# Query rows split into two 16-bit halves and turned by DMA instead of on TensorE, in an attention and feed-forward kernel

## The chip, the cores and the metric

The kernel runs on one core of one Trainium2 chip. The metric is the device time of one execution in microseconds (us), the median of several runs. The engines are TensorE (PE, with its weight loads listed as PEld), VectorE (DVE), ScalarE (ACT), GpSimd (POOL) and SyncE (SP), which only issues transfers here.

## The reference, cut to what matters

```python
# 4 batches of 256 rows, D = 256; context: 4 batches of 1601 rows
q = (xn @ wq).reshape(B, L, 16, 128)        # xn: layer norm of x
k, v = xn @ wk, xn @ wv                     # 4 key/value heads of 128
q, k, k_ctx = rms_norm(q), rms_norm(k), rms_norm(ctx @ wk_ctx)
q, k = rope(q), rope(k)                     # rotary embedding, own rows alone
scores = q @ concat(k_ctx, k).T * scale + causal_mask
out = softmax(scores) @ concat(v_ctx, v) @ wo
# then x + out, a quantised feed-forward part, a second attention, a mixture of experts
```

All products are wanted at more than 16-bit accuracy, so the kernel holds each operand as the sum of a high and a low float16 part (names ending in _h and _l) and makes a product from three matmuls.

## The kernel before

**Groups and units.** The attention of the first layer is worked off in 16 groups (batch times key/value head, `NG`). A group has 8 units (`UNITS`): 4 heads times 2 tiles of 128 query rows. One unit is 128 query rows of one head against 1601 context keys and 128 or 256 own keys. In unit u of a group TensorE makes the scores of unit u + 2 (`qk`, lines 1217 to 1219 called with `qT_h`, `kT_h`) and the product with the values of unit u (`pv`, lines 1365, 1366 and 1369). In between stands the softmax: DVE takes the row maximum (`chunk_max` line 1722, `row_max` lines 1728 and 1730), ACT takes the exponential (`exp`, line 1517), ACT and POOL round it to the high half (`p_hi`, POOL's `split_last`), DVE and POOL subtract to get the low half (`p_lo`, line 1742), and SP turns both halves by DMA (`turn`, lines 1157 and 1160, target `pT_h` and `pT_l`).

**Jobs.** The operands of the next group are made between these steps. `JOBS_AT` is a list written out by hand: for each unit the jobs that run in it, in order. `("piece", p)` projects two tiles of context (or the own rows: pieces 0 and 1 are the query rows of the two tiles, 2 the own keys and values, 3 the last 65 context rows). `("kq", s)` turns normalised rows on TensorE as float32 transposes through PSUM; steps 1 to 3 are 512 context keys each, 4 the last 65, 5 the own 256 keys, 0 and 6 the query rows of tile 0 and 1 (line 1307). ACT then copies the high half from PSUM (`kq_hi_part`, line 1504) and DVE subtracts the low half (`kq_lo_part`, lines 1716 and 1718). `("out", i)` is the output projection of the group before. On PE the first job of a unit comes before the scores, the others after them; on ACT two jobs come after `p_hi` and the rest behind; on DVE the first job stands between the two halves of `p_lo`, the second after them, the rest behind.

**PSUM banks.** Jobs take three banks in turn (`XBS`), so a job waits on PE until the third job before it has been read out (`bank_user`, `wait_bank`). All engines run in program order; there is no other scheduler.

**POOL** normalises the rows and applies the rotary embedding (`POOL_AT`): the query rows of tile 0 in unit 0, those of tile 1 in units 1 and 2, own keys in unit 3, context keys behind.

**SP's queue** carries, in program order, the two turns of each unit, and between them loads for the weights of later stages (`lane_load` after unit 0, one load after unit 3, two stores of 128 KB after unit 7). The context of two of the four batches is held in SBUF; the other two wait in DRAM, and `bring_back` reloads one of them at the end of group 2 and one at the end of group 6, as two transfers of 800 KB each.

Before the groups there is a preparation phase (`PREP_JOBS`, the jobs of group 0, with rotary embedding and norms on DVE), before that the context summary of the second layer, and behind the groups a tail of about 200 us which the change does not touch.

Of the kernel before, what the change touches and what calls it, by code (L numbers as in the profile page):

```python
# [63 lines left out]
KQ_STEPS = 7  # L64
# [11 lines left out]
OUT_JOBS = [j for j in JOB_LIST if j[0] == "out"]  # L76
# [5 lines left out]
KQ_AT = {s: [j for j in PREP_JOBS if j[0] == "kq"].index(("kq", s)) for s in range(KQ_STEPS)}  # L82
# [91 lines left out]
def build(nc, x, ctxT, wq, wk, wv, wo, wk_ctx, wv_ctx, q_norm, k_norm, w_gateT, w_upT, w_downT,  # L174
# [3 lines left out]
    with ExitStack() as ctx:  # L178
# [73 lines left out]
        sq = sm("sq", [P, 2, REP, DH], BF16)  # L252
# [3 lines left out]

        kT_h = sm("kT_h", [P, 2, KEY_COLS], F16)
# [113 lines left out]
        ot_tr, ot_hi, ot_lo, oj_mm, x1_done = (sem(n) for n in ("ot_tr", "ot_hi", "ot_lo", "oj_mm", "x1_done"))  # L371
        dve_step, act_step = sem("dve_step"), sem("act_step")
# [98 lines left out]

        def squares_at(p):

            return sum(piece_slots(k) for k in range(p))
# [14 lines left out]
        def kq_view(s, kT, qT, par, bank):  # L489

            if s in (0, 6):
                lt = s // 6
                return qT[:, par, lt * REP:(lt + 1) * REP, :].rearrange("p h n -> p (h n)"), PS[:, bank, :], False
# [8 lines left out]

        def prep_bank(n):
            return PREP_BANKS[n % len(PREP_BANKS)]

        def job_bank(job):
            return XBS[JOB_LIST.index(job) % len(XBS)]
# [12 lines left out]

        def bank_user(job, g):

            kind, i = job
            if kind == "mean":
                return (("kq", 3), NG - 1) if i == 0 else (("mean", 0), g)
            at = JOB_LIST.index(job) - len(XBS)
            while g >= 0:
                if at < 0:
                    at, g = at + len(JOB_LIST), g - 1
                elif runs(JOB_LIST[at], g):  # L530
                    return JOB_LIST[at], target(JOB_LIST[at], g)
                else:
                    at -= len(XBS)
            return None
# [53 lines left out]
        def run_job(g, job, kinds):  # L588

            kind, i = job  # L590
            if kind == "mean":
                kinds[kind](i)
            elif kind == "out":
                kinds[kind](i, target(job, g), job_bank(job))
            else:
                to = target(job, g)
                kinds[kind](i, to, to % 2, job_bank(job))
# [530 lines left out]
        def _(sp):  # L1128
# [32 lines left out]

            def group(g, last=False):
                for u in range(UNITS):
                    turn(g, u)
                    if u == 0 and 0 < g < NG - 1:
                        lane_load(g)
                    if u == LANE_AT + 1 and g < NG - 1:
                        sp.wait_ge(lane_sum, g + 1)
                        sp.dma_start(piece_f.rearrange("p (c n) -> p c n", c=kept_sources[g].shape[1]), kept_sources[g])\
                          .then_inc(pw_in, 16)  # L1170
                    if u == UNITS - 1 and g < NG - 1:
                        sp.wait_ge(pw_lo, g + 1)
                        for k, t in enumerate((piece_h, piece_l)):
                            sp.dma_start(kept_w[k, :, g * KEPT:(g + 1) * KEPT], t).then_inc(pw_kept, 16)
# [14 lines left out]
            def bring_back(slot, groups_done):  # L1189

                sp.wait_ge(pc_mm, NP * groups_done)
                for k, t in enumerate((ctx_h, ctx_l)):
                    sp.dma_start(t[:, slot, :, :].rearrange("p c n -> p (c n)"), kept[slot, k, :, :])\
                      .then_inc(ctx_moved, 16)

            lane_load(0)
            for g in range(NG):
# [13 lines left out]
        def _(pe):  # L1211
# [61 lines left out]
            def piece(p, g, par, bank=XB):  # L1273

                b, kv = g // KVH, g % KVH
                kind = PIECES[p]
                if p == KV_PIECES[0]:
                    pe.wait_ge(ctx_moved, 64 + 64 * (g // (2 * KVH)))
                if kind in ("q0", "q1"):
                    lt = int(kind[1])  # L1280
                    jobs = [(PS[:, bank, :], xT_h, xT_l, (b * L + lt * P), P, wsf_h, wsf_l, 0, 512)]
                elif kind == "self":
                    jobs = [(PS[:, bank, lt * 256:lt * 256 + 256], xT_h, xT_l, (b * L + lt * P), P, wsf_h, wsf_l, 512, 256)
                            for lt in range(LT)]
                elif kind == "rem":
                    jobs = [(PS[0:CREM, bank, 0:256], None, None, (CT - 1) * P, CREM, wc_h, wc_l, 0, 256)]
                else:
                    jobs = [(PS[:, bank, j * 256:j * 256 + 256], None, None, (2 * kind[1] + j) * P, P, wc_h, wc_l, 0, 256)
                            for j in range(2)]
                for o, ah, al, col, n, bh, bl, w0, wn in jobs:  # L1290
                    for c in range(DC):
                        if ah is None:
                            lhs = (ctx_h[:, ds(b % SLOTS, 1), c, col:col + n].rearrange("p a n -> p (a n)"),
                                   ctx_l[:, ds(b % SLOTS, 1), c, col:col + n].rearrange("p a n -> p (a n)"))
                        else:
                            lhs = (ah[:, c, ds(col, n)], al[:, c, ds(col, n)])
                        last = three(o, lhs, (bh[:, c, kv, w0:w0 + wn], bl[:, c, kv, w0:w0 + wn]),
                                     c == 0, c == DC - 1)
                last.then_inc(pc_mm, 1)

            def transpose_kq(s, g, par, bank=XB):

                if s in (0, 6):
                    lt = s // 6
# [33 lines left out]
            def qk(g, u, c, par):  # L1338
# [43 lines left out]
            kinds = {"out": out_proj, "piece": piece, "kq": transpose_kq, "mean": mean}  # L1382
            turn, rotate, turn_first, tail = tail_pe(pe, three)

            def group(g, par, first, last):
                for u in range(UNITS):
# [19 lines left out]
                    if last and u == UNITS - 1:  # L1406
# [4 lines left out]
                        out_proj(0, NG - 1, job_bank(("out", 0)))  # L1411
# [8 lines left out]
            for n, (kind, i) in enumerate(PREP_JOBS):  # L1420
                if n == 2:
                    pe.wait_ge(l1_R, B)
                if n >= len(PREP_BANKS):
                    wait_bank(pe, PREP_JOBS[n - len(PREP_BANKS)], 0)
                to = 1 if n == len(PREP_JOBS) - 1 else 0
                kinds[kind](i, to, to, prep_bank(n))
# [9 lines left out]
            for i, before in ((1, (("out", 3), NG - 2)), (2, (("out", 0), NG - 1)), (3, (("out", 1), NG - 1))):  # L1436
                wait_bank(pe, *before)
                out_proj(i, NG - 1, job_bank(("out", i)))
# [4 lines left out]
        def _(act):  # L1443
# [39 lines left out]
            def piece_out(p, g, par, bank=XB):  # L1483
# [5 lines left out]
                wait(act, pc_copy, pieces_done(p, g) - 2)  # L1489
                act.wait_ge(pc_mm, pieces_done(p, g))  # L1490
                rows, w = (CREM if kind == "rem" else P), (DH if q else 2 * DH)
                for j in range(piece_slots(p)):
                    act.activation(sq[0:rows, p % 2, j, :], PS[0:rows, bank, j * w:j * w + DH], ACT.Square,  # L1493
# [45 lines left out]
            kinds = {"out": out_hi_part, "piece": piece_out, "kq": kq_hi_part,  # L1539
# [11 lines left out]
            def group(g, par, first, last):  # L1551

                for u in range(UNITS):
# [16 lines left out]
                    else:  # L1570
# [3 lines left out]
                        out_hi_part(0, NG - 1, job_bank(("out", 0)))  # L1574
# [18 lines left out]
            out_hi_part(1, NG - 1, job_bank(("out", 1)))  # L1593
# [4 lines left out]
        def _(dve):  # L1598
# [111 lines left out]

            def kq_lo_part(s, g, par, bank=XB):
# [80 lines left out]
            kinds = {"out": out_lo_part, "piece": piece_lo, "kq": kq_lo_part,  # L1792
# [14 lines left out]
            def group(g, par, first, last):  # L1807
                for u in range(UNITS):
# [18 lines left out]
                    if last and u == UNITS - 1:  # L1827
                        lo_part(0, 0, 0)
                        lo_part(0, 0, 1)
                        out_lo_part(0, NG - 1, job_bank(("out", 0)))  # L1830
# [50 lines left out]
            for i in range(1, 2 * LT):  # L1881
                out_lo_part(i, NG - 1, job_bank(("out", i)))
# [192 lines left out]
```

## Time and profile before

| | |
|---|---|
| median of 3 runs | 1298.2 us (1294.91 to 1299.37) |
| the profiled execution | 1299.34 us, its span 1297.5 us |
| PE busy | 1193.7 us, 92% of the span |
| PE weight loads busy | 893.8 us, 69% |
| DVE busy | 1015.4 us, 78% |
| ACT busy | 832.3 us, 64% |
| POOL busy | 790.8 us, 61% |
| mean granted TensorE clock | 0.976 |
| hardware DMA queue | 56.5% of the 16 engines |
| chain that ended last | PE 69%, DVE 16%, DMA 5% |

The profile is one execution taken by the hardware profiler. Matmuls are pipelined: a matmul's recorded duration is longer than the distance to the next one, so costs on PE are read from the distances between starts. The idle time in brackets at the end of a timeline line is the engine's idle time before that instruction, with what released it.

### The profile page before, as it was taken

To read this page: it belongs to the slowest core of one execution; us is meant where nothing else is said; L and a number is where in the kernel's file an instruction comes from. 1 tells how busy PE (TensorE), PEld (TensorE's weight loads), DVE (VectorE), ACT (ScalarE), POOL (GpSimd) and SP (SyncE) were. 2 spreads that over 40 slices of the span, in tenths; PEclk is the share of its full clock that TensorE was granted. 3 is DMA by queue.
4 is the path that set the end of the run, shared out by engine and by line. 5 is a ranking of instruction groups with operands and counts; after the bars stand their busy time and mean duration, and the time that the engine had idled before them with its cause. 6 is when DMAs were issued, how large, how long until landed. Compare 5 with 4: busy or idle time off the path is not lost.

```text
span 1297.5 us, 30487 instructions
## 1 busy us (share of the span) xinstructions
PE 1193.7 (92%) x11547; PEld 893.8 (69%) x11547; DVE 1015.4 (78%) x1979; ACT 832.3 (64%) x1917; POOL 790.8 (61%) x1010
## 2 busy tenths in 40 slices
PE   4998699999999999999999999999999976777898
PEld 2544477877787777778777777777777765455557
DVE  6876768888688888788888878888888887776673
ACT  4755567776677676767677677777777644446431
POOL 2765386867668585857668595857768533761000
PEclk9998999999999999999999999999999998789999
DMA  8620067576867687695767677676778898000000
GB/s 286 201 82 15 18 137 163 129 159 134 187 135 154 143 148 149 128 209 130 159 132 152 145 148 147 133 160 139 151 145 153 161 193 222 1 1 1 1 1 33
DMA packets 507298, 164.94 MB, mean 127 GB/s; under 512 B 485488, under 2 KB 500352, under 8 KB 506896
## 3 DMA queue, kind: packets, MB, share of 16 engines
q1 hardware_dynamic: 506128, 159.57, 56.5%
q0 software_dynamic: 1024, 3.42, 1.0%
q8 instruction: 92, 1.51, 0.5%
q14 instruction: 54, 0.44, 0.1%
HBM read 33.05 MB, written 8.26 MB: 32 GB/s over the span
## 4 chain that ended last, share of the span: by engine, by line
PE 69%; DVE 16%; DMA 5%; POOL 3%; ACT 3%; issue 3%; SPq 2%; POOLq 0%; DVEq 0%; ACTq 0%
PE PS L1217 14%; PE PS L1219 13%; PE PS L1218 13%; PE PS L1369 7%; PE PS L1365 7%; PE PS L1366 7%; DVE mx L1722 5%; DVE pl L1742 3%; DMA pT_l<-pl 2%; DMA pT_h<-ph 2%; PE PS L1318 1%; PE PS L706 1%; PE PS L684 1%; DMA sin<-in_c_sin 1%; DVE f_s L1653 1%
## 5 line engine op out<-in xcount | busy, mean ns | idle before, releaser
L1722 DVE TENSOR_REDUCE mx<-PS 128x1 f32<-128x512 f32 (+2 forms) x512 | 296.5, 622 | 123.8 <-PE PS L1219 122.6
L1365 PE MATMUL PS<-v_h,pT_h 128*128 128x129 f16 (+1 forms) x1856 | 225.8, 222 | 9.9 <-DMA pT_h<-ph 9.9
L1959 POOL CAST ph<-pr_end 128x705 f16<-128x705 f32 (+1 forms) x128 | 109.9, 858 | 200.4 <-ACT pr_end L1517 200.4
L1366 PE MATMUL PS<-v_l,pT_h 128*128 128x128 f16 (+1 forms) x1856 | 225.8, 221 | 0.0
L1365 PEld LDWEIGHTS PS<-v_h,pT_h 128*128 128x128 f16 (+1 forms) x1856 | 182.7, 98 | 14.0 <-DMA pT_h<-ph 11.3
L1217 PE MATMUL PS<-kT_h,qT_h 128*128 128x512 f16 (+2 forms) x512 | 181.9, 355 | 7.6 <-ACT pr L1517 7.6
L1517 ACT ACTIVATE pr<-PS,nb 128x1024 f32<-128x1024 f32 x128 | 144.0, 1125 | 68.9 <-DVE nb L1730 68.9
L1366 PEld LDWEIGHTS PS<-v_l,pT_h 128*128 128x128 f16 (+1 forms) x1856 | 183.0, 99 | 2.4
L1218 PE MATMUL PS<-kT_l,qT_h 128*128 128x512 f16 (+2 forms) x512 | 181.0, 354 | 0.0
L1219 PE MATMUL PS<-kT_h,qT_l 128*128 128x512 f16 (+2 forms) x512 | 180.8, 353 | 0.0
L1742 DVE TENSOR_TENSOR pl<-pr,ph 128x1024 f16<-128x1024 f32 x128 | 169.3, 1322 | 0.0
L1493 ACT ACTIVATE sq<-PS 128x128 bf16<-128x128 f32 (+1 forms) x368 | 98.9, 283 | 81.3 <-PE PS L1219 81.0
L1369 PE MATMUL PS<-v_h,pT_l 128*128 128x129 f16 (+1 forms) x1856 | 131.6, 222 | 6.7 <-DMA pT_l<-pl 6.6
L1444 ACT ACTIVATE ph<-pr 128x1024 f16<-128x1024 f32 x128 | 135.5, 1059 | 0.0
L1369 PEld LDWEIGHTS PS<-v_h,pT_l 128*128 128x128 f16 (+1 forms) x1856 | 114.5, 98 | 8.6 <-DMA pT_l<-pl 8.4
L1517 ACT ACTIVATE pr_end<-PS,nb 128x705 f32<-128x705 f32 (+1 forms) x128 | 117.4, 917 | 3.6 <-DVE pl L1742 3.6
L1217 PE MATMUL PS<-wc_h,ctx_h 128*128 128x256 f16 (+1 forms) x416 | 113.4, 273 | 3.8 <-DVE v_l L1708 3.4
L1219 PE MATMUL PS<-wc_h,ctx_l 128*128 128x256 f16 (+1 forms) x416 | 113.3, 272 | 0.0
L1218 PE MATMUL PS<-wc_l,ctx_h 128*128 128x256 f16 (+1 forms) x416 | 113.3, 272 | 0.0
L1742 DVE TENSOR_TENSOR pl<-pr_end,ph 128x512 f16<-128x512 f32 x128 | 107.9, 843 | 0.3 <-issue 0.3
L1444 ACT ACTIVATE o_s<-PS,rden 128x128 f32<-128x128 f32 x128 | 48.1, 376 | 91.5 <-DVE rden L1757 91.0
L1932 POOL TENSOR_TENSOR rs<-rs,mhalf 128x4 f32<-128x4 f32 (+2 forms) x100 | 101.7, 1016 | 7.8
(287 smaller groups left out, 2964.4 us busy)
## 6 DMA issues: line engine op xcount, KB each, us to landing
stage<-in_ctxT SPq DMA_DIRECT2D x8, 800.5 KB, 6.6
weights_kept<-relay SPq DMA_DIRECT2D x30, 128.0 KB, 2.3
relay<-in_w_lanes SPq DMA_DIRECT2D x14, 204.9 KB, 3.6
stage<-in_wq SPq DMA_DIRECT2D x4, 512.0 KB, 4.0
stage<-in_wo SPq DMA_DIRECT2D x4, 512.0 KB, 3.8
pT_h<-ph SPq DMA_TRANSPOSE x128, 3.6
pT_l<-pl SPq DMA_TRANSPOSE x128, 3.6
ctx_kept<-ctx_h SPq DMA_DIRECT2D x2, 800.5 KB, 8.1
```

What stands on the lines that cost most here:

```text
L1217: mm(o, ah, bh, start=start, stop=False)
L1218: mm(o, ah, bl, start=False, stop=False)
L1219: return mm(o, al, bh, start=False, stop=stop)
L1365: mm(PS[:, OB, 0:DH + 1], pT_h[0:rows, slot, t, :], v_h[0:rows, par, v, :], start=t == 0, stop=False)
L1366: mm(PS[:, OB, 0:DH], pT_h[0:rows, slot, t, :], v_l[0:rows, par, v, :], start=False, stop=False)
L1369: last = mm(PS[:, OB, 0:DH + 1], pT_l[0:rows, slot, t, :], v_h[0:rows, par, v, :], start=False, stop=t == len(tiles) - 1)
L1444: copy = lambda o, i, scale=1.0: act.activation(o, i, ACT.Copy, scale=scale)
L1517: act.activation(o, i, ACT.Exp, bias=nb[:, slot:slot + 1], scale=SCALE).then_inc(exp_done, 1)
L1722: dve.reduce_max(mx[:, c:c + 1], PS[:, c, 0:cols(u % LT, c)], AX_X).then_inc(mx_part, 1)
L1742: dve.tensor_tensor(pl[:, slot, at], src, ph[:, slot, at], ALU.subtract).then_inc(p_lo_made, 1)
L1932: last = pool.tensor_tensor(rs[:, 0:n], rs[:, 0:n], mhalf[:, 0:n], ALU.pow)
L1959: pool.tensor_copy(ph[:, slot, HALF:LAST + w], pr_end[:, 0:BANK + w]).then_inc(pool_hi, 1)
```

## The change

- **Query turns.** The jobs `("kq", 0)` and `("kq", 6)` are gone; in their places stand `("q", 0)` in unit 2 and `("q", 1)` in unit 4 instead of unit 3. A q job does nothing on PE. ACT copies the 128x512 float32 query rows to `qn_h` (float16), DVE subtracts to `qn_l`, and SP turns both with a DMA transpose into `qT_h` and `qT_l`, behind the turns of unit 3 and of unit 5. There is one `qn_h` and one `qn_l`: ACT waits before it overwrites them until the turns of the other tile have landed (`turned_q`). The first scores of each tile wait for `turned_q` on PE.
- **Own keys.** `("kq", 5)` moves from the end of unit 3 to the head of unit 4, and `("piece", 9)` comes behind the scores in unit 4.
- **Banks.** A group now has 19 jobs with a bank instead of 21, so the three banks rotate from group to group; each job still waits for the third before it.
- **Context reload.** `bring_back` becomes four transfers of 400 KB, one each behind units 0 to 3 of groups 3 and 7. The wait for them on PE now asks for the reload that the batch needs.
- **Squares.** The scratch tile `sq` becomes single, with a wait for the previous piece's copy (ACT's own), and a query piece waits until `qn_l` of the last use is made.

```diff
-           [("piece", 5), ("kq", 0), ("piece", 6)],
-           [("piece", 7), ("kq", 6), ("piece", 8), ("kq", 5)],
-           [("piece", 9), ("kq", 4), ("kq", 1)],
+           [("piece", 5), ("q", 0), ("piece", 6)],
+           [("piece", 7), ("piece", 8)],
+           [("kq", 5), ("piece", 9), ("kq", 4), ("q", 1), ("kq", 1)],
            [("kq", 2), ("kq", 3)],
...
+            def turn_queries(lt, g):
+                par = g % 2
+                sp.wait_ge(q_lo, g * LT + lt + 1)
+                for t, rows in ((qT_h, qn_h), (qT_l, qn_l)):
+                    sp.dma_start_transpose(t[:, par, lt * REP:(lt + 1) * REP, :], rows[:, :]).then_inc(turned_q[lt], 16)
...
                     turn(g, u)
+                    if u in (3, 5) and not last:
+                        turn_queries(u // 2 - 1, g + 1)
...
+                    if g in (KVH - 1, 2 * KVH - 1) and u < 2 * DC:
+                        bring_back(g // KVH, u)
...
+            def bring_back(slot, part):
+
+                if part == 0:
+                    sp.wait_ge(pc_mm, NP * KVH * (slot + 1))
+                t, c = (ctx_h, ctx_l)[part // DC], part % DC
+                sp.dma_start(t[:, slot, c, :], kept[slot, part // DC, :, c * SC:(c + 1) * SC]).then_inc(ctx_moved, 16)
...
-                if g in (KVH - 2, 2 * KVH - 2):
-                    bring_back(g // KVH, (g // KVH + 1) * KVH)
...
-                    pe.wait_ge(ctx_moved, 64 + 64 * (g // (2 * KVH)))
+                    pe.wait_ge(ctx_moved, 64 * max(1, g // KVH))
...
-                if s in (0, 6):
-                    lt = s // 6
-                    pe.wait_ge(rope_done, g * len(ROPES) + ROPES.index(f"q{lt}1") + 1)
-                    for j in range(REP):
-                        last = pe.transpose(PS[:, bank, j * P:(j + 1) * P], qr[:, lt * REP + j, :], ident[:, :])
-                elif s == 4:
+                if s == 4:
...
-                    pe.wait_ge(kq_lo, kq_done([[0, 1], [2], [3], [4, 5]][c], g))
-                if u == 1 and c == 0:
-                    pe.wait_ge(kq_lo, kq_done([6], g))
+                    pe.wait_ge(kq_lo, kq_done([[1], [2], [3], [4, 5]][c], g))
+                if u < LT and c == 0:
+                    pe.wait_ge(turned_q[u], 32 * (g + 1))
...
+            def q_hi_part(lt, g, par, bank=None):
+                n = g * LT + lt
+                act.wait_ge(rope_done, g * len(ROPES) + ROPES.index(f"q{lt}1") + 1)
+                wait(act, turned_q[1 - lt], 32 * ((n + 1) // 2))
+                copy(qn_h[:, :], query_rows(lt)).then_inc(q_hi, 1)
...
+            def q_lo_part(lt, g, par, bank=None):
+                dve.wait_ge(q_hi, g * LT + lt + 1)
+                dve.tensor_tensor(qn_l[:, :], query_rows(lt), qn_h[:, :], ALU.subtract).then_inc(q_lo, 1)
```

## Rows read from the trace of the kernel before

**Rows 1.** The page's part 1: busy time, share of the span, instructions, by engine.
```profile
PE 1193.7 (92%) x11547; PEld 893.8 (69%) x11547; DVE 1015.4 (78%) x1979; ACT 832.3 (64%) x1917; POOL 790.8 (61%) x1010
```

**Rows 2.** Windows: length, busy us by engine, granted clock, DMA share, GB/s.
```profile
400.00:500.00 100.00, 98.76 (x1063) 78.83 (x1061) 83.15 (x160) 73.85 (x193) 76.58 (x99) 1.00 0.71 145
...
337.00:347.00 10.00, 7.02 (x63) 5.79 (x62) 3.84 (x6) 5.46 (x19) 9.16 (x14) 0.83 0.93 200
```

**Rows 3.** PE's waits over the whole run: releaser, us in total, times, longest.
```profile
PE PS L1365 <- DMA pT_h<-ph: 9.9, 4, 4.4
...
PE PS L1314 <- DVE v_l L1708: 7.8, 15, 0.6
```

**Rows 4.** DVE's timeline (start, duration): the lane sum, once per group, unit 2.
```profile
297.90 1.27 DVE L1747 TENSOR_REDUCE relay<-relay 48x1 f32<-48x1094 f32 x1
...
360.40 1.27 DVE L1747 TENSOR_REDUCE relay<-relay 48x1 f32<-48x1094 f32 x1
...
476.20 1.27 DVE L1747 TENSOR_REDUCE relay<-relay 48x1 f32<-48x1094 f32 x1
...
534.06 1.27 DVE L1747 TENSOR_REDUCE relay<-relay 48x1 f32<-48x1094 f32 x1
...
593.84 1.27 DVE L1747 TENSOR_REDUCE relay<-relay 48x1 f32<-48x1094 f32 x1
```

**Rows 5.** PE's timeline, unit 2 of group 6: query transposes and the next job.
```profile
529.88 0.61 PE L1307 MATMUL PS<-ident,qr 128*128 128x128 f32 x4
530.33 0.27 PE L1217 MATMUL PS<-wc_h,ctx_h 128*128 128x256 f16 x1
```

**Rows 6.** Groups by form, whole run: count, busy us, mean ns, idle before.
```profile
L1742 DVE TENSOR_TENSOR pl<-pr_end,ph 128x512 f16<-128x512 f32 x128 | 107.9, 843 | 0.3 <-issue 0.3
...
L1718 DVE TENSOR_TENSOR qT_l<-PS,qT_h 128x512 f16<-128x512 f32 x32 | 21.7, 679 | 0.0
...
L1307 PE MATMUL PS<-ident,qr 128*128 128x128 f32 x128 | 19.5, 274 | 0.0
L1504 ACT ACTIVATE qT_h<-PS 128x512 f16<-128x512 f32 x32 | 19.1, 598 | 22.7 <-PE PS L1307 22.7
...
L1444 ACT ACTIVATE relay<-relay 128x512 f16<-128x512 f32 x15 | 9.3, 622 | 0.0
```

**Rows 7.** PE's timeline, units 3 to 5 of group 6.
```profile
539.41 0.27 PE L1219 MATMUL PS<-wc_h,ctx_l 128*128 128x256 f16 x1
540.31 0.44 PE L1314 MATMUL PS<-ident,kr 128*128 128x128 f32 x2 [0.62 <-DVE v_l L1708]
...
546.72 0.23 PE L1310 MATMUL PS<-ident,kr 65*128 65x65 f32 x1
...
549.64 0.60 PE L1318 MATMUL PS<-ident,kr 128*128 128x128 f32 x4
550.08 0.38 PE L1217 MATMUL PS<-kT_h,qT_h 128*128 128x512 f16 x1
```

**Rows 8.** DVE's timeline, unit 4 of group 6: first job, second half of p_lo.
```profile
548.49 0.42 DVE L1708 SCALAR_TENSOR_TENSOR v_l<-PS,v_h 128x256 f16<-128x256 f32 x1
548.82 1.22 DVE L1742 TENSOR_TENSOR pl<-pr,ph 128x1024 f16<-128x1024 f32 x1
```

**Rows 9.** ACT's timeline, units 4 and 5 of group 6.
```profile
545.54 0.40 ACT L1444 ACTIVATE v_h<-PS 128x256 f16<-128x256 f32 x1
546.98 1.14 ACT L1504 ACTIVATE kT_h<-PS,wcol 128x65 f16<-128x65 f32 x2 [1.04 <-PE PS L1310]
...
548.53 1.11 ACT L1517 ACTIVATE pr<-PS,nb 128x1024 f32<-128x1024 f32 x1
```

**Rows 10.** SP's timeline: turns behind the first context reload, and undisturbed ones.
```profile
330.01 4.70 SPq L1157 DMA_TRANSPOSE pT_h<-ph  x1
334.81 5.24 SPq L1160 DMA_TRANSPOSE pT_l<-pl  x1
...
533.57 1.31 SPq L1160 DMA_TRANSPOSE pT_l<-pl  x1
...
537.12 1.49 SPq L1157 DMA_TRANSPOSE pT_h<-ph  x1
```

**Rows 11.** The page's part 6: turns of the low halves, median us to landing.
```profile
pT_l<-pl SPq DMA_TRANSPOSE x128, 3.6
```

More of the change, by code:

```diff
@@ L75 @@
 JOB_LIST = [j for jobs in JOBS_AT for j in jobs]
-OUT_JOBS = [j for j in JOB_LIST if j[0] == "out"]
+RING = [j for j in JOB_LIST if j[0] != "q"]
 PREP_JOBS = [("piece", 0)] + [j for j in JOB_LIST if j[0] != "out"]
@@ L81 @@
 TERNARY_AT = {1: 0, 2: 1, 3: 2}
-KQ_AT = {s: [j for j in PREP_JOBS if j[0] == "kq"].index(("kq", s)) for s in range(KQ_STEPS)}
+KQ_AT = {s: [j for j in PREP_JOBS if j[0] == "kq"].index(("kq", s)) for s in range(1, KQ_STEPS + 1)}
 KV_PIECES = [p for p in range(NP) if PIECES[p] not in ("q0", "q1")]
@@ L251, in build @@
         qr = sm("qr", [P, UNITS, DH], F32)
-        sq = sm("sq", [P, 2, REP, DH], BF16)
+        sq = sm("sq", [P, REP, DH], BF16)
         ss = sm("ss", [P, 2 * REP + LT + CT], F32)
@@ L255, in build @@
         rot = sm("rot", [P, 2, 2, DH], F32)
+        qn_h = sm("qn_h", [P, BANK], F16)
+        qn_l = sm("qn_l", [P, BANK], F16)
         kT_h = sm("kT_h", [P, 2, KEY_COLS], F16)
@@ L371, in build @@
         ot_tr, ot_hi, ot_lo, oj_mm, x1_done = (sem(n) for n in ("ot_tr", "ot_hi", "ot_lo", "oj_mm", "x1_done"))
+        q_hi, q_lo = sem("q_hi"), sem("q_lo")
+        turned_q = [sem(f"turned_q{lt}") for lt in range(LT)]
         dve_step, act_step = sem("dve_step"), sem("act_step")
@@ L470, in piece_slots, with query_rows @@
             return {"q0": REP, "q1": REP, "self": LT, "rem": 1}.get(PIECES[p], 2)
+        def query_rows(lt):
+            return qr[:, lt * REP:(lt + 1) * REP, :].rearrange("p h n -> p (h n)")
         def squares_at(p):
@@ L501, in build, with prep_user, job_bank @@
         PREP_BANKS = [TB, TB + 1, OB, XB]
+        prep_at = [sum(k != "q" for k, _ in PREP_JOBS[:n]) for n in range(len(PREP_JOBS))]
         def prep_bank(n):
-            return PREP_BANKS[n % len(PREP_BANKS)]
-        def job_bank(job):
-            return XBS[JOB_LIST.index(job) % len(XBS)]
+            return PREP_BANKS[prep_at[n] % len(PREP_BANKS)]
+        def prep_user(n):
+            if PREP_JOBS[n][0] == "q" or prep_at[n] < len(PREP_BANKS):
+                return None
+            return [j for j in PREP_JOBS if j[0] != "q"][prep_at[n] - len(PREP_BANKS)]
+        def job_bank(job, g):
+            if job[0] == "q":
+                return None
+            if g >= NG - 1:
+                return XBS[job[1] % LT]
+            return XBS[(g * len(RING) + RING.index(job)) % len(XBS)]
         def target(job, g):
@@ L519, in runs, with user_from, last_user @@
             return target(job, g) < NG
+        def user_from(at):
+            while at >= 0:
+                g, job = at // len(RING), RING[at % len(RING)]
+                if runs(job, g):
+                    return job, target(job, g)
+                at -= len(XBS)
+            return None
+        def last_user(bank):
+            end = (NG - 1) * len(RING)
+            return user_from(max(at for at in range(end - len(XBS), end) if XBS[at % len(XBS)] == bank))
         def bank_user(job, g):
             kind, i = job
+            if kind == "q":
+                return None
             if kind == "mean":
[L525 to L534, printed above, removed]
+                return last_user(MB) if i == 0 else (("mean", 0), g)
+            if g == NG - 1:
+                return last_user(XBS[i % LT]) if i < LT else (("out", i - LT), g - 1)
+            return user_from(g * len(RING) + RING.index(job) - len(XBS))
         def unit_no(g, u):
@@ L593, in run_job @@
             elif kind == "out":
-                kinds[kind](i, target(job, g), job_bank(job))
+                kinds[kind](i, target(job, g), job_bank(job, g))
             else:
                 to = target(job, g)
-                kinds[kind](i, to, to % 2, job_bank(job))
+                kinds[kind](i, to, to % 2, job_bank(job, g))
         def second(hf, j):
@@ L1187, in bring_weights @@
                     at += n
[L1189 to L1194, printed above, removed]
+            def bring_back(slot, part):
[3 more added lines that the diff above has]
+                sp.dma_start(t[:, slot, c, :], kept[slot, part // DC, :, c * SC:(c + 1) * SC]).then_inc(ctx_moved, 16)
             lane_load(0)
+            for lt in range(LT):
+                turn_queries(lt, 0)
             for g in range(NG):
                 group(g, g == NG - 1)
-                if g in (KVH - 2, 2 * KVH - 2):
-                    bring_back(g // KVH, (g // KVH + 1) * KVH)
             bring_weights()
@@ L1380, in mean @@
                     mm(PS[:, MB, 0:NTERN], ones[0:1, :], lsum[:, 3 * LANES:], start=True, stop=True).then_inc(lane_b, 1)
-            kinds = {"out": out_proj, "piece": piece, "kq": transpose_kq, "mean": mean}
+            kinds = {"out": out_proj, "piece": piece, "kq": transpose_kq, "q": lambda lt, g, par, bank=None: None, "mean": mean}
             turn, rotate, turn_first, tail = tail_pe(pe, three)
@@ L1422, in _ @@
                     pe.wait_ge(l1_R, B)
-                if n >= len(PREP_BANKS):
-                    wait_bank(pe, PREP_JOBS[n - len(PREP_BANKS)], 0)
+                if prep_user(n):
+                    wait_bank(pe, prep_user(n), 0)
                 to = 1 if n == len(PREP_JOBS) - 1 else 0
@@ L1437, in _ @@
                 wait_bank(pe, *before)
-                out_proj(i, NG - 1, job_bank(("out", i)))
+                out_proj(i, NG - 1, job_bank(("out", i), NG))
             tail()
@@ L1488, in piece_out @@
                 wait(act, pc_norm, pieces_done(p, g) - NP)
-                wait(act, pc_copy, pieces_done(p, g) - 2)
+                wait(act, pc_copy, pieces_done(p, g) - 1)
+                if q:
+                    wait(act, q_lo, g * LT + int(kind[1]) - LT + 1)
                 act.wait_ge(pc_mm, pieces_done(p, g))
@@ L1492, in piece_out @@
                 for j in range(piece_slots(p)):
-                    act.activation(sq[0:rows, p % 2, j, :], PS[0:rows, bank, j * w:j * w + DH], ACT.Square,
+                    act.activation(sq[0:rows, j, :], PS[0:rows, bank, j * w:j * w + DH], ACT.Square,
                                    scale=1 / (WS * float(np.sqrt(DH))), accum_out=ss[0:rows, at + j:at + j + 1])
@@ L1537, in weight_piece_hi @@
                 copy(piece_h, piece_f, WS).then_inc(pw_hi, 1)
-            kinds = {"out": out_hi_part, "piece": piece_out, "kq": kq_hi_part,
+            kinds = {"out": out_hi_part, "piece": piece_out, "kq": kq_hi_part, "q": q_hi_part,
                      "mean": lambda i: None}
@@ L1573, in group @@
                         hi_part(0, 0, 1)
-                        out_hi_part(0, NG - 1, job_bank(("out", 0)))
+                        out_hi_part(0, NG - 1, job_bank(("out", 0), NG))
                     while todo:
@@ L1592, in _ @@
             copy_first(0, 1)
-            out_hi_part(1, NG - 1, job_bank(("out", 1)))
+            out_hi_part(1, NG - 1, job_bank(("out", 1), NG))
             tail()
@@ L1791, in ternary @@
                 dve.scalar_tensor_tensor(home, w[:, :], at[0], helper[:, :], ALU.is_gt, ALU.subtract).then_inc(done, 1)
-            kinds = {"out": out_lo_part, "piece": piece_lo, "kq": kq_lo_part,
+            kinds = {"out": out_lo_part, "piece": piece_lo, "kq": kq_lo_part, "q": q_lo_part,
                      "mean": mean}
@@ L1829, in group @@
                         lo_part(0, 0, 1)
-                        out_lo_part(0, NG - 1, job_bank(("out", 0)))
+                        out_lo_part(0, NG - 1, job_bank(("out", 0), NG))
                         quantise(0, True)
@@ L1881, in _ @@
             for i in range(1, 2 * LT):
-                out_lo_part(i, NG - 1, job_bank(("out", i)))
+                out_lo_part(i, NG - 1, job_bank(("out", i), NG))
             tail()
```

7 lines of the change are left out of this document (2 added, 5 removed).

## The prediction

> **What bounds the kernel now.** I read the busy shares first, then windows of 100 us, then PE's waits, then one group in the timelines. PE is busy for 92% of the span [rows 1], and in a window inside the groups for 98.8 us of 100 at the full clock of 2.4 GHz, while DVE has 83.2 and ACT 73.9 [rows 2]. So through the 16 groups PE is the bound, and what its program order loses to waits is small: 7.8 us before the own-key transposes of line 1314 (15 times, at most 0.6 each) and 9.9 us in four waits for turned probabilities [rows 3]. The lane sum of DVE comes once a group and serves as a clock: 534.06 - 476.20 = 57.9 us for an undisturbed group, but 360.40 - 297.90 = 62.5 us and 593.84 - 534.06 = 59.8 us for the two groups in which the context is reloaded [rows 4]. So the reloads cost 4.6 + 1.9 = 6.5 us in all. The reader should see both in the rows: PE sets the 57.9, the transfers the surplus. But PE is not alone at the limit everywhere. In units 3 to 5 the next instruction that PE needs from DVE or ACT is ready only a few tenths before it is used, and that decides how much of a saving on PE arrives.
>
> **Part 1, the query transposes leave PE.** Four transposes start at 529.88 and the next job at 530.33, so they hold PE for 0.45 us [rows 5]; two such jobs per group give 0.9 us. There are 128 transposes in 32 such jobs [rows 6], 30 of them inside groups 0 to 14, where PE is the bound, and two in the preparation. Full worth inside the groups: 15 x 0.9 = 13.4 us. The preparation waits for DVE and POOL there, not for PE; I cost and credit nothing, with 1 us either way.
>
> The VectorE page of the Trainium skill (VectorE: DVE Perf Modes, "The three transpose paths" and "Rules for kernel authors") speaks against this part: it gives 390 ns for a 128x128 transpose on TensorE and 1309 ns by DMA, and advises TensorE where PSUM will do. By its figure the eight transposes would be worth 3.1 us a group to PE; the rows show 0.11 us each in a stream, and a turn of 14 or 15 such blocks landing in 3.6 us, so its figures are those of single transposes and not used.
>
> **Part 2, what ACT, DVE and SP get instead.** The ACT copy came from PSUM at 598 ns; from SBUF the same shape took 622 ns [rows 6]: no change. The DVE subtraction took 679 ns with PSUM as a source; with both sources in SBUF the same shape takes 843 ns on average [rows 6]: 0.16 us more, twice a group, on an engine with 17% to spare. SP issues four more turns per group. No row shows a turn of four blocks; it lies between 0.4 us (4/14.5 of an issue of 1.3 to 1.5) and a whole issue of 1.5 us [rows 10]. I take 0.5, nearest to the block count, since the issue time does follow the width there (1.31 and 1.49). Even 3 us for a pair fits behind the turns of unit 3, which are issued at 533.57, before the next turn at 537.12 [rows 10] and behind those of unit 5, where the queue is free until unit 6. Two new waits stand in queues. On ACT the copy of tile 1 waits until the turns of tile 0 have landed; behind it are the copy of key step 1 and the exponential of unit 6. Tile 0's rows are low-halved near 534.1, turned by about 536, landed by about 540 with 3.6 us [rows 11], and wanted near 546.5: 6 us of cover. On PE the first scores of the next group wait for the turns; tile 0 has more than 10 us there, tile 1 (low half near 548.5, landed by 554) some 8.
>
> **Part 3, the own-key step moves.** Today line 1314 waits because its bank is that of piece 7: piece 8 ends at 539.41 + 0.11 = 539.52 and the transposes begin at 540.31, a gap of 0.79 us [rows 7], of which the profile counts 0.62 as idle. Over all groups the idle sum of 7.8 [rows 3] plus this 0.17 each makes 0.7 us a group. At the head of unit 4 its bank is that of piece 6, long free: this gap goes, 0.7 us. What is late next: key step 1 now needs the bank that the own-key step has just used, two jobs earlier in the same unit. DVE serves the unit's first job between the halves of p_lo. Today that is piece 9's low half, done at 548.49 + 0.42 = 548.91, that is 2.2 us after the scores ended at 546.72 [rows 7, 8], and 0.06 more until PE starts. In the new order PE has only piece 9 (12 matmuls at 0.11 = 1.31 us) and the 65-key step (0.06) between the end of the scores and key step 1, so it waits 2.25 - 1.37 = 0.9 us. The gap of 0.7 is thus traded for one of 0.9.
>
> Then ACT. Piece 9 moves behind the scores on PE, so ACT meets it 0.28 us after its end: with piece 8 as the start, PE's new times are own keys to 541.4, scores to 543.7, piece 9 to 545.0, ACT's piece 9 from 545.3, 1.2 us. Then come the 65-key copy 0.3, the query copy 0.55, the key copy 0.65 and the weight piece 0.6, and the exponential of unit 6 starts at 548.4 and is done at 549.5 (it took 1.11 [rows 9]). PE has meanwhile done key step 1 (546.0 to 546.45), the values (2.4 us, from the distance 546.72 to 549.64 less 0.5) and key step 2 (0.44), and is at 549.3. It waits another 0.2 us; from 0.1 to 0.4 by how the ACT instructions overlap. Today the same exponential is ready at 549.64 for scores that begin at 550.08 [rows 7, 9].
>
> Sum for a group: -0.9 - 0.7 + 0.9 + 0.15 = -0.55 us. As a check, absolute: today's scores of unit 7 begin at 550.08, with tile 0's 0.45 us saved already before unit 3, and in the new order at 549.5. Times 15 groups: -8.3 us. From there on PE has no new wait: DVE is ready for unit 0's maxima at 557.1 against scores due at 557.0.
>
> **Part 4, the reload in four parts.** Today's turns behind the reload are held 4.70 and 5.24 us in SP's queue instead of 1.5 [rows 10], PE runs dry (7.0 of 10 us) and the clock falls to 0.83 in that window [rows 2]. In parts each turn has 400 KB before it, a quarter, so its delay is about a quarter of the 3.2 + 3.7 us, 1.7 us; the high halves of units 1 to 4 are issued some 9 us before PE wants them (537.12 issued, wanted after 546.72). Hidden; I credit 5.5 of the 6.5 us, with bounds of 2 and 6.5. The later wait for the reload has all four parts landed units before.
>
> The squares' wait is on ACT's own earlier instruction, the query piece's wait on a low half 20 us old, and the banks' rotation keeps the distance of three: nothing.
>
> **Total.** -8.3 - 5.5 = -13.8 us. Against the profiled execution's own 1299.3 us that is 1285.5; this execution stands 1.1 us above the median of 1298.2, so 1284.4, and I say 1285.
>
> **Rivals.** (a) PE stays the bound throughout: the two new waits do not arise, because DVE and ACT run earlier than in my walk. Then 13.4 + 15 x 0.7 + 6.5 = 30 us, 1268; half of it 1277. For it: DVE and ACT are idle by a sixth and a quarter [rows 2]. Against it: the old gap is of the same kind and did arise, with the same DVE order. (b) The work moved into unit 4 costs all that PE saves: ACT and DVE have all of the own keys, piece 9, tile 1 and key step 1 there; a further 0.55 us before the exponential cancels parts 1 and 3, and only the reload is left: 1298.2 - 5.5 = 1293, with 1290 for half. (c) Slower: the query turns land late. ACT's copy of tile 1 waits for tile 0's turns, and the exponential of unit 6 stands behind it. It costs only if they take over 10 us instead of 4 (536 to 546.5), and decides once the delay passes 0.55 + 5.5/15 = 0.9 us a group. At 2 us a group the time is 1298 + 15 x (2 - 0.55) - 5.5 = 1314. For it: the queues are busy for 0.71 of the time [rows 2], and turns behind the 1.6 MB did take 5 us to issue [rows 10]. Against it: undisturbed turns land in 3.6 us [rows 11]. By the figures of the page named above, a pair of four-block turns would take 8 x 1.3 = 10.5 us, just this point. (d) The reload in parts does not hide, and each part delays PE by about 1 us: only 8.3 - 1 us gained, 1291.
>
> **How the numbers follow.** The walk as made, 1281 to 1289: 0.43. (a) 0.2, of which half above 1274. (b) 0.19. (d) 0.08. (c) 0.06. A mixture of small costs elsewhere that ends within 0.3%: 0.04. A measurement of this kernel can tell about 0.3%, 4 us, from no change. Faster by more than that: all of the first, (a), most of (b), (d): 0.84; same 0.09; slower 0.07. The range reaches from the middle of (a) to the end of (b): 1274 to 1295.
>
> **What would show it.** The group clock (lane sum to lane sum) at 57.3 us instead of 57.9, and the two reload groups within 0.5 us of it. No idle before line 1314's successor; a new idle of 0.6 to 0.9 us a group on PE before key step 1, released by DVE's own-key low half, and 0 to 0.4 before the scores of unit 7, released by ACT. Query turns landing in 2 to 4 us. DVE's new subtraction near 0.8 us. What would make it wrong: no wait at key step 1 (then (a)), an idle before the scores of over 0.7 us a group (then (b)), waits on the query turns (then (c)).

## Result and the profile after

The changed kernel takes 1284.88 us (median of 4 runs, 1283.05 to 1286.68) against 1298.78 us for the kernel before (4 runs), 13.9 us less. The measured ratio is 0.9879, 95% interval 0.9849 to 0.9909; that of the two medians alone is 0.9893. In a second measurement the ratio was 0.9902 (0.9882 to 0.9921). The profiled execution took 1283.05 us, its span 1281.2 us, 16.3 us less than that of before; the rows below are from it. Line numbers have moved: 1217 to 1219 are now 1254 to 1256, 1314 and 1318 are 1346 and 1350, 1365 and 1369 are 1397 and 1401, the lane sum is 1791, ACT's exponential 1557.

Part 1 of the page, busy time by engine, answers [rows 1]:

```profile
PE 1174.8 (92%) x11419; PEld 878.0 (69%) x11419; DVE 1030.4 (80%) x1979; ACT 823.5 (64%) x1917; POOL 805.6 (63%) x1010
```

PE has lost its 128 transposes and 19 us of recorded busy time. DVE has 15 us more and POOL 15 us more, though POOL was given no new work. Of DVE's 15 us the new subtraction is 5.7 (32 times 856 ns instead of 679):

```profile
L1753 DVE TENSOR_TENSOR qn_l<-qr,qn_h 128x512 f16<-128x512 f32 x32 | 27.4, 856 | 0.0
```

The rest lies in subtractions that were there before and now take longer, `p_lo` 1373 and 862 ns instead of 1322 and 843. What slows them is not shown here; it comes back below, where 0.2 us of it decide how long PE waits.

DVE's timeline of the lane sum, the group clock of [rows 4], around the first reload (start, duration):

```profile
296.46 1.28 DVE L1791 TENSOR_REDUCE relay<-relay 48x1 f32<-48x1094 f32 x1
352.78 1.27 DVE L1791 TENSOR_REDUCE relay<-relay 48x1 f32<-48x1094 f32 x1
...
467.32 1.27 DVE L1791 TENSOR_REDUCE relay<-relay 48x1 f32<-48x1094 f32 x1
...
524.56 1.27 DVE L1791 TENSOR_REDUCE relay<-relay 48x1 f32<-48x1094 f32 x1
```

An undisturbed group takes 524.56 - 467.32 = 57.24 us instead of 57.9, and the stretch in which the first reload used to stand takes 56.3 instead of 62.5. Part of that 56.3 is the clock's own: the lane sum of this group came 0.9 us late against PE, so the stretch before it reads 58.5. From own-key step to own-key step on PE it is 57.2 us (302.77 to 359.96), where it was 62.3 (304.15 to 366.48). The sum over all groups is hardly touched by this. From the first lane sum to the last, 14 groups, it is 800.3 us instead of 815.4: 15.1 of the 16.3 us of span lie there.

PE's waits in the groups (190 to 990 us; releaser, total, times, longest), first of the kernel before, then of the changed one, and PE's timeline of units 4 and 5 of one group, beside [rows 7]:

```profile
PE PS L1314 <- DVE v_l L1708: 7.2, 14, 0.6
PE PS L1365 <- DMA pT_h<-ph: 4.8, 2, 3.0
PE PS L1369 <- DMA pT_l<-pl: 1.2, 3, 0.8
```

```profile
PE PS L1350 <- DVE kT_l L1762: 12.3, 14, 1.2
PE PS L1401 <- DMA pT_l<-pl: 0.4, 2, 0.2
```

```profile
478.29 0.22 PE L1342 MATMUL PS<-ident,kr 65*128 65x65 f32 x1
479.39 0.66 PE L1350 MATMUL PS<-ident,kr 128*128 128x128 f32 x4 [0.88 <-DVE kT_l L1762]
481.47 0.99 PE L1401 MATMUL PS<-v_h,pT_l 128*128 128x129 f16 x14
482.29 0.60 PE L1350 MATMUL PS<-ident,kr 128*128 128x128 f32 x4
482.73 0.38 PE L1254 MATMUL PS<-kT_h,qT_h 128*128 128x512 f16 x1
```

The wait before the own keys (line 1314) is gone. So are the two waits for turned high halves, at 340 and 575 us, just behind the two reloads: 4.8 of the reloads' 6 us. In its place PE idles 0.9 us before key step 1, once a group, until DVE has made the own keys' low half, and nowhere else to speak of. By the distances between starts, which the prediction counts in, the gap is 479.39 - (478.29 + 0.06) = 1.04 us, and the old one was 0.79. The scores of unit 7, at 482.73, follow key step 2 without a wait. How close ACT is can be read from its timeline there:

```profile
479.81 0.66 ACT L1476 ACTIVATE qn_h<-qr 128x512 f16<-128x512 f32 x1
480.33 0.71 ACT L1544 ACTIVATE kT_h<-PS,wcol 128x512 f16<-128x512 f32 x1
480.90 0.67 ACT L1476 ACTIVATE relay<-relay 128x512 f16<-128x512 f32 x1
481.42 1.15 ACT L1557 ACTIVATE pr<-PS,nb 128x1024 f32<-128x1024 f32 x1
```

The exponential ends at 482.57, 0.16 us before PE comes for it. Four copies (65-key, query, key, weight piece) run from 479.62 on without a pause ahead of it.

### The profile page after: what moved, and what is told of

Same layout as the page of the kernel before. It is cut to its first block, busy times and chain, and to the rows that moved or that the text cites. A ratio compares the mean times of both kernels' runs of the same rounds, so it can differ in the third digit from the quotient of the medians.

```text
span 1281.2 us, 30330 instructions
## 1 busy us (share of the span) xinstructions
PE 1174.8 (92%) x11419; PEld 878.0 (69%) x11419; DVE 1030.4 (80%) x1979; ACT 823.5 (64%) x1917; POOL 805.6 (63%) x1010
## 3 DMA queue, kind: packets, MB, share of 16 engines
q8 instruction: 91, 1.49, 0.5%
## 4 chain that ended last, share of the span: by engine, by line
PE 73%; DVE 15%; DMA 3%; POOL 3%; ACT 3%; issue 3%; SPq 0%; POOLq 0%; DVEq 0%; ACTq 0%
PE PS L1254 15%; PE PS L1256 14%; PE PS L1255 14%; PE PS L1401 8%; PE PS L1397 7%; PE PS L1398 7%; DVE mx L1766 5%; DVE pl L1786 3%; DMA pT_l<-pl 2%; PE PS L1350 2%; PE PS L733 1%; PE PS L711 1%; DMA blk<-in_c_blk 1%; PE PS L1359 1%; DVE f_s L1693 1%
## 5 line engine op out<-in xcount | busy, mean ns | idle before, releaser
L1786 DVE TENSOR_TENSOR pl<-pr,ph 128x1024 f16<-128x1024 f32 x128 | 175.8, 1373 | 0.0
L2006 POOL TENSOR_TENSOR pl<-pr_end,ph 128x193 f16<-128x193 f32 (+1 forms) x128 | 92.5, 723 | 19.1 <-POOL ph L2003 0.9
```

Of the source, the lines that this page charges most:

```text
L1786: dve.tensor_tensor(pl[:, slot, at], src, ph[:, slot, at], ALU.subtract).then_inc(p_lo_made, 1)
```

## Experiments

a1, e1, e2 and e4 ran on one chip, e3, e5, e6 and e7 on a second, e8 and e9 on a third, each lot with its own runs of the kernel before (medians 1299.62, 1299.95 and 1302.12 us). The ratios given are to the kernel before on the same chip. Where e3 and e5 to e9 are set beside a1, the ratios and the lane sums are the fair comparison. "Lane sums" is the time from the first lane sum of the profiled execution to the last, 14 groups: 815.4 us before.

**a1: the changed kernel again**, as the reference of what follows.

> The changed kernel itself, timed again beside the three that follow, so that they can be compared on one chip. Its ratio to the kernel before should be 0.988 to 0.991.

1287.63 us, ratio 0.9902 (0.9882 to 0.9921). Its lane sums span 800.1 us, within 0.3 of the first profile, though its whole span is 8.7 us longer: 2.0 us of that lie before the first lane sum and 6.8 behind the last. There one wait for a turned probability took 6.4 us, at 1025 us, where the same wait in the first profile took 1.8; the late turn stands in SP's queue behind the two stores of 128 KB after group 14. So the lane sums are the sharper of the two measures, and I read both.

**e1: the reload whole, in the changed kernel.** `bring_back` and its place in SP's queue as before, the rest as changed:

```diff
-                    if g in (KVH - 1, 2 * KVH - 1) and u < 2 * DC:
-                        bring_back(g // KVH, u)
...
+                if g in (KVH - 2, 2 * KVH - 2):
+                    bring_back(g // KVH, (g // KVH + 1) * KVH)
```

> The changed kernel, but the context is reloaded as before: two transfers of 800 KB at the end of groups 2 and 6. My theory: the reload in four parts is worth 5.5 to 6.5 us, so this is 5 to 6.5 us slower than the changed kernel (ratio to before 0.993), and the group clock shows one group some 4 us and one some 2 us longer, with turned probabilities late on PE. The rival: the reload in parts is hidden no better and the gain comes from elsewhere; then this is within 1 us of the changed kernel.

1291.78 us, ratio 0.9937 (0.9919 to 0.9956): 4.2 us slower than a1 by the medians. The lane sums span 806.1 instead of 800.1, 6.0 us more, with one long group:

```profile
527.57 1.27 DVE L1791 TENSOR_REDUCE relay<-relay 48x1 f32<-48x1094 f32 x1
...
590.46 1.28 DVE L1791 TENSOR_REDUCE relay<-relay 48x1 f32<-48x1094 f32 x1
```

62.9 us for the second reload and 59.2 for the first (before: 59.8 and 62.5). Which of the two costs more has changed round, and nothing here shows why. 6.0 us by the lane sums is within the 5 to 6.5 expected, 4.2 by the medians is below it. Against the kernel before, e1 has parts 1 to 3 alone: its lane sums are 9.3 us less.

**e2: the reload in four parts, alone**, in the kernel before.

> The kernel before with the reload in four parts as its only edit. My theory: 5.5 to 6.5 us faster than before (ratio 0.9955), with the undisturbed group still at 57.9 us. The rival, that the parts fit only because the new order leaves room behind them: under 3 us faster.

1292.43 us, ratio 0.995 (0.9933 to 0.9968): 6.5 us faster by the ratio, 7.2 by the medians. Its lane sums span 808.9 us, 6.4 less than before, and every group from the third on takes 57.8 to 58.2 us. The parts need no room that the new order makes. Parts 1 to 3 alone (e1, 9.3 us) and part 4 alone (6.4) make 15.8, and both together gave 15.1: they add up to within 0.7 us.

**e3: own keys back at the end of unit 3.**

```diff
-           [("piece", 7), ("piece", 8)],
-           [("kq", 5), ("piece", 9), ("kq", 4), ("q", 1), ("kq", 1)],
+           [("piece", 7), ("piece", 8), ("kq", 5)],
+           [("piece", 9), ("kq", 4), ("q", 1), ("kq", 1)],
```

> The changed kernel with the own-key step back at the end of unit 3, query turns unchanged. In the changed kernel piece 8 is off PE at 471.9 and POOL ends the rotary embedding of the own keys at 473.3. My theory: the bank wait of before does not return (its bank is now that of piece 6), but PE waits 1.3 us for POOL here, and the wait of 0.9 us at key step 1 goes; so the group clock is 57.4 to 57.7 against 57.25 and the run is 2 to 6 us slower than the changed kernel. The rival, that the wait at key step 1 is a loss which the move of the own-key step made: faster than the changed kernel by 10 us or more.

1292.4 us, ratio 0.994 (0.9917 to 0.9963), 5 us slower than a1 by the ratios; an undisturbed group takes 57.7 us and the lane sums span 804.5, 4.4 more. The wait at key step 1 went and a larger one came, released by POOL's rotary embedding of the own keys (waits of PE, 190 to 990 us):

```profile
PE PS L1346 <- POOL kr L1995: 14.9, 11, 1.4
```

It stands in 11 of the 13 own-key steps of this stretch; in groups 2 and 6 PE lost less than 0.25 us there. So the move of the own-key step is worth 0.45 us in an undisturbed group although it brings a wait of 0.9. What it avoids is not the bank, which is piece 6's in either place once the query job is gone, but POOL, which is not ready when PE comes early.

**e4: key step 1 to the head of unit 5.**

```diff
-           [("kq", 5), ("piece", 9), ("kq", 4), ("q", 1), ("kq", 1)],
-           [("kq", 2), ("kq", 3)],
+           [("kq", 5), ("piece", 9), ("kq", 4), ("q", 1)],
+           [("kq", 1), ("kq", 2), ("kq", 3)],
```

> The changed kernel with key step 1 moved from the end of unit 4 to the head of unit 5, so that its bank (that of the own-key step) has been free for 2 us. The trace of the changed kernel shows 0.9 us of idle on PE before key step 1 in each group, which should go. My theory says PE is the bound with this wait on top, but ACT stands close behind: the exponential of unit 6 starts at 481.42 in group 5 and PE comes for it at 482.74 with 0.2 us to spare; without the gap PE would come at 481.7, ACT 0.7 us earlier by one key copy less, so 0.4 to 0.8 us a group remain, 6 to 12 us over 15 groups: ratio to before 0.980 to 0.985. The rival, that ACT or DVE bounds units 4 and 5: no gain beyond 2 us, and a new idle of 0.7 us before the scores released by ACT.

1281.15 us, ratio 0.9848 (0.9827 to 0.987), 6.5 us faster than a1 by the medians. By the group clock the gain was less than expected: 57.0 us a group, 0.25 less, and 3.7 us over 14 groups. PE's and ACT's timelines show the wait moved, not removed:

```profile
481.16 0.60 PE L1350 MATMUL PS<-ident,kr 128*128 128x128 f32 x4
482.45 0.39 PE L1254 MATMUL PS<-kT_h,qT_h 128*128 128x512 f16 x1 [0.69 <-ACT pr L1557]
```

```profile
480.74 0.66 ACT L1476 ACTIVATE relay<-relay 128x512 f16<-128x512 f32 x1
481.25 1.14 ACT L1557 ACTIVATE pr<-PS,nb 128x1024 f32<-128x1024 f32 x1
```

PE has done key step 1 at 481.16 + 0.44 = 481.6 by the distance between starts and gets the exponential at 482.4.

**e5: e4 with the weight piece one unit on** (`PIECE_HI_AT, PIECE_LO_AT = 5, 6` instead of 4, 5).

> The kernel of e4 with the weight piece moved one unit on as well (ACT's half from unit 4 to 5, DVE's from 5 to 6). In e4 the group clock is 57.0 us and PE waits 0.69 us a group for ACT's exponential, which starts at 481.25 straight behind the weight piece (0.5 to 0.6 us). My theory, that ACT's order alone sets this wait: it goes, the clock falls to 56.3 or 56.4, ratio to before 0.976 to 0.979. The rival, that DVE is the limit behind ACT: the wait stays and is released by DVE's row maximum; clock 57.0, ratio 0.984.

1276.57 us, ratio 0.9802 (0.9779 to 0.9825), where I had expected 0.976 to 0.979: 23 us faster than before by the medians, 26 by the ratio. Its lane sums span 791.9 us, 8.2 less than a1's. The group clock is 56.5 to 56.6, a little above my 56.3 to 56.4, and the wait for ACT is down to this (190 to 990 us, at most 0.2 each):

```profile
PE PS L1254 <- ACT pr L1557: 2.4, 14, 0.2
```

So ACT's order had set nearly all of it (0.69 us a group in e4, 0.17 now); DVE, with 87 of 100 us busy, was not the limit. PE is now busy for 99.7 us of the window from 400 to 500.

**e6: no query turns after the second group**, so later groups work on old queries. ACT's copies and DVE's subtractions for them stay.

> The changed kernel with the queries turned for the first two groups alone, so that later groups use old queries: it leaves out 56 of the 64 query turns and all waits on them. My theory: the turns are wholly covered, so nothing changes in the group clock (57.25, within 0.1) and in the time (within 2 us of the changed kernel). The rival, that SP's queue or the DMA engines, now busy for 63% instead of 56.5%, cost PE something: faster than the changed kernel by 4 us or more.

1287.92 us, ratio 0.9899 (0.9881 to 0.9917); group clock 57.3, lane sums over 800.3 us. No difference from a1 in either: the turns, their waits and the added DMA traffic (0.79 of the DMA engines from 400 to 500 us in the changed kernel, 0.72 here) cost nothing that can be seen.

**e7: 12 more matmuls a group on PE.**

```diff
-                for o, ah, al, col, n, bh, bl, w0, wn in jobs:
+                for o, ah, al, col, n, bh, bl, w0, wn in jobs[0:1] * (p in (6, 8) and g > 0) + jobs:
```

> The changed kernel with 12 more matmuls of 256 columns a group on PE: pieces 6 and 8 of groups 1 to 15 make their first tile twice, the second time over the first. That is 12 x 0.109 = 1.31 us of PE a group, in the two units from which the query transposes were taken, 19.6 us over 15 groups. My theory, PE is the bound: the group clock rises by 1.2 to 1.3 us to 58.5, and the time by 17 to 20 us. The rival, that the transposes were worth little and the gain came from the new order: under 8 us.

1303.64 us, ratio 1.0026 (1.0012 to 1.004): 16 us slower than a1, a little less than the 17 to 20 expected; group clock 58.5, lane sums over 816.9 us, 16.9 more. Between the lane sums lie 14 groups, so 14 x 1.31 = 18.3 us were put in there. The rest is in PE's own waits (190 to 990 us):

```profile
PE PS L1350 <- DVE kT_l L1762: 9.9, 14, 0.7
```

2.4 us less idle than in the changed kernel, 0.17 a group: DVE has more time before PE comes. The distances between PE's starts over one undisturbed group show the same: 1.31 us put in, 0.17 less before key step 1, 0.06 more behind the other key steps, together the 1.2 us that the group is longer. PE's time counts fully except for what a wait takes up.

**e8: one transpose of four, in the order of before.**

```diff
-                    for j in range(REP):
+                    for j in range(REP if g == 0 else 1):
```

> The kernel before with one instead of four TensorE transposes in each query job after the first group, all else as it was; it leaves out the other three, so three heads in four get wrong queries. PE loses 6 x 0.11 = 0.67 us of work a group, 10 us over 15 groups. My theory: half of it arrives. The job in unit 2 is a clean saving of 0.33 us; the one in unit 3 stands between the scores and the own-key step, which waits for a release of DVE that is timed from the scores, so its 0.33 us only lengthens that wait (from 0.6 to 0.9 us at most). Group clock 57.5 to 57.6 against 57.9, 4 to 6 us faster. The rival, PE's work alone counts: clock 57.2, 10 us faster.

1294.94 us, ratio 0.995 (0.9932 to 0.9968), 6.5 us faster than before by the ratio and 7.2 by the medians, a little over the 4 to 6 expected; lane sums over 808.4, 7.0 less; undisturbed groups 57.5 to 57.6 us. As forecast, half of the 0.67 us a group arrived. But the row shows another releaser than I had named (waits of PE, 190 to 990 us):

```profile
PE PS L1314 <- POOL kr L1951: 9.6, 10, 1.0
PE PS L1314 <- DVE v_l L1708: 3.0, 4, 1.1
```

In most groups it is now POOL's own-key embedding that ends the wait, 0.24 us after DVE. In the kernel before it was done well ahead: POOL's last step of it in group 6 of the kernel before, and in group 5 of e8, where PE begins the own keys at 540.31 and 478.29:

```profile
538.64 0.73 POOL L1951 TENSOR_TENSOR kr<-rot 128x256 f32<-128x256 f32 x1
```

```profile
476.93 1.21 POOL L1951 TENSOR_TENSOR kr<-rot 128x256 f32<-128x256 f32 x1
```

It ended 0.94 us before PE began there, and 0.15 here: PE comes earlier, and the step itself took longer (nothing here shows why). e3 met the same releaser.

**e9: a third turn of one block** in each query job.

> The changed kernel with a third turn in each query job, of one block of 128 columns into a spare tile. In the changed kernel a turn of four blocks holds SP's queue for 1.26 us and one of 14 or 15 blocks for 1.3 to 1.5, where I had expected 0.5 for four. Theory A, a fixed cost of nearly 1.2 us and little by size: the one-block turn takes 1.1 to 1.25 us. Theory B, a cost by size with a floor set by something that is in flight in front of it: the one-block turn takes under 0.7 us. In either case the group clock stays within 0.1 us of 57.25, since there are 2 us of cover behind these turns, and the time within 3 us of the changed kernel.

1285.79 us, ratio 0.9885 (0.9859 to 0.9911), group clock 57.3: covered. SP's timeline, first the kernel with the third turn:

```profile
469.62 1.29 SPq L1194 DMA_TRANSPOSE qT_h<-qn_h  x1
470.97 1.26 SPq L1194 DMA_TRANSPOSE qT_l<-qn_l  x1
472.27 1.24 SPq L1195 DMA_TRANSPOSE spare<-qn_h  x1
```

and the changed kernel, a turn of 15 blocks of unit 3 and the pair behind it, with part 6 of that kernel's page (median us to landing; 3.6 for both in the kernel before) below:

```profile
466.82 1.52 SPq L1187 DMA_TRANSPOSE pT_l<-pl  x1
468.39 1.30 SPq L1193 DMA_TRANSPOSE qT_h<-qn_h  x1
469.74 1.26 SPq L1193 DMA_TRANSPOSE qT_l<-qn_l  x1
```

```profile
pT_h<-ph SPq DMA_TRANSPOSE x128, 4.1
pT_l<-pl SPq DMA_TRANSPOSE x128, 3.6
```

As theory A had it: one block 1.24 us, four 1.26, fifteen 1.5. The cost in the queue is nearly fixed.

## Why the prediction was right, point by point

- **PE is the bound in the groups.** Right: of the 18.3 us that e7 puts in, 16.9 arrive, and a wait that is 2.4 shorter takes up the rest. e8 shows the condition that goes with it: in the old order only half of a saving arrives, because what PE saves between the scores and the own-key step is waited out again.
- **Part 1, 0.9 us a group.** Right as a term of PE's work. Neither e7 nor e8 measures it alone: the first works in the new order, the second in the old. But the distances between PE's starts close the account of an undisturbed group: -0.9 for the transposes, -0.79 for the old gap, +1.04 for the new one is -0.65 us, against 57.24 - 57.9 by the group clock, and no other distance has changed by more than 0.06.
- **Part 2, DVE and ACT.** DVE's subtraction took 856 ns on average (843 foreseen), in single cases 0.68, 1.0 or 1.3 us; ACT's copy took 679 ns instead of 622.
- **Part 2, SP's queue.** The turns were mis-sized: 1.26 to 1.30 us of SP's queue for nearly each and not 0.5. The step that failed is a reading of [rows 10]: the issue time was said to follow the width, 1.31 against 1.49 us, but the turn of 1.31 us is that of unit 3, with 15 blocks, and the one of 1.49 that of unit 4, with 14. Nor does a pair of 3 us fit before unit 4's turn: the turn at 533.57 holds the queue until 534.88, which leaves 2.2 us before 537.12. In the changed kernel the pair takes 2.6 us, a load follows it, and unit 4's high half is issued at 471.74, 1.4 us after it was ready; in the kernel before and in e6 it is issued 0.02 us after. It cost nothing because PE comes for that half only at 479.88 (e6 and e9 show the same clock). Landing took 2.5 us, so tile 0 is there at 472.2, 4.8 us after its low half.
- **The page on transposes.** The Trainium skill (VectorE: DVE Perf Modes, "The three transpose paths") gives 1309 ns for one block by DMA. By an estimate from that a pair of four-block turns would take 10.5 us. The measured pair is issued and landed within 1.3 + 2.5 = 3.8 us, so the figure does not add up over blocks.
- **Part 3, a gap of 0.7 for one of 0.9.** Right in place and releaser: a gap of 0.79 was traded for one of 1.04. Its details were not all right. The new gap is 0.15 us longer than in my walk, because DVE's first part of `p_lo` ahead of the own keys took 0.87 us and not 0.69:

```profile
547.88 0.69 DVE L1742 TENSOR_TENSOR pl<-pr_end,ph 128x512 f16<-128x512 f32 x1
```

```profile
478.13 0.87 DVE L1786 TENSOR_TENSOR pl<-pr_end,ph 128x512 f16<-128x512 f32 x1
478.93 0.41 DVE L1762 TENSOR_TENSOR kT_l<-PS,kT_h 128x256 f16<-128x256 f32 x1
```

The wait of 0.15 before the scores of unit 7 did not arise: I had ACT ready 0.2 us after PE, it was ready 0.16 us before. That these two cancel is luck. What is left, -0.65 instead of -0.55 us, is that the old gap of an undisturbed group was 0.79 and not the mean of 0.7. And I had not walked POOL: the own-key step was moved for its bank, but its bank was free in either place, and what the move avoids is the wait for POOL (e3).

- **Part 4, 5.5 of 6.5 us.** Right: by the lane sums 6.0 (e1) and 6.4 (e2), so the credit was 0.5 to 1 us low. The medians scatter more widely around it: 4.2 and 7.2.
- **Sum.** Over the 14 groups between lane sums, (57.9 - 57.24) x 14 = 9.2 us by the group clock and 8.7 (15.1 - 6.4) to 9.3 (e1) by the lane sums, against 8.3 foreseen for 15; with the reload 15.1 to 13.8. The medians give 13.9; in the second measurement 12.
- **Rivals.** (a) needed the new wait not to arise; it arose in all 14 groups looked at. (b) did not come true, but it is right about what limits further gains: ACT's exponential was ready only 0.16 us before PE came for it, and in e4 PE waits for it. (c) is refuted by e6 and (d) by e1 and e2.

A version that beats both kernels is e5, at 0.9802: the new wait at key step 1 can be avoided if ACT's copy of the weight piece leaves unit 4 together with that step.

## What to carry to other kernels

In this kernel, where one engine is busy almost without a break, a saving on it arrived in full only where no wait stood behind it; where another engine, timed from an earlier point, released the next step, the saving was waited out there (e8: half of it). So walk the order from the edit to the next two or three waits, with the releaser of each and whoever stands close behind it: here a gap of 0.79 us was traded for one of 1.04, and taking that one away showed ACT 0.7 us behind. Split a large reload into parts placed behind steps with slack: four parts of 400 KB cost nothing that could be seen in e2 and at most 0.6 us a reload in the changed kernel, two of 800 KB in a row 6 us for both reloads together.

## What the hardware showed that was not expected

A DMA transpose held SP's queue for nearly the same time whatever its size: 1.24 us for one block of 128x128 float16, 1.26 to 1.30 for four, and mostly 1.47 for 14 and 1.52 for 15, with a few at 1.3 and single ones up to 3.4 (e9 and the changed kernel). Small turns were therefore dear in the queue. The same subtraction on DVE, 128x512 with both sources in SBUF, took 0.68, 1.0 or 1.3 us from one group to the next, and 0.2 us more in the first part of `p_lo` lengthened PE's one wait. And the end of this kernel varies by itself: two executions of the changed kernel with group clocks alike differed by 8.7 us in span, 4.6 of it in one turn that came late behind two stores (waits of 6.4 and 1.8 us).
